# Differential attention in a two-layer kernel: two heads' value products interleaved in the two column halves, transposes and products in two parts, one order per engine

## The reference, cut to what matters

```python
def _L1_attn_ref(x, Wq, Wkv, Wout, lambda_q1, ..., gamma):      # H = 8, D = 32, B = 4, T = 1024
    q = (x @ Wq).reshape(B, T, 2 * H, D).transpose(0, 2, 1, 3) * scaling
    k, v = jnp.split(x @ Wkv, 2, axis=-1)                        # k: 2H heads of 32, v: H heads of 64
    dots = jnp.einsum('bhqd,bhkd->bhqk', q, k)
    attn_w = jax.nn.softmax(dots, axis=-1).reshape(B, H, 2, T, T)
    attn_w = attn_w[:, :, 0] - lam * attn_w[:, :, 1]
    attn = jnp.einsum('bhqk,bhkd->bhqd', attn_w, v)
    rms = jnp.sqrt(jnp.mean(attn * attn, axis=-1, keepdims=True))
    attn = gamma * (attn / (rms + EPS)) * (1.0 - LAMBDA_INIT)
    return attn.transpose(0, 2, 1, 3).reshape(B, T, 2 * H * D) @ Wout
```

## Time and profile before

| | us |
|---|---|
| median of 3 runs | 2968.69 (2963.91 to 2975.45) |
| the profiled execution | 2971.7, of which 2969.5 are the span of the trace |
| mean granted clock of TensorE | 0.886 of 2.4 GHz |
| PE busy | 2382.1 (80% of the span) |
| DVE busy | 2111.1 (71%) |
| ACT busy | 1700.0 (57%) |
| POOL busy | 1430.3 (48%) |

### The profile page before, as it was taken

The page is one execution under the profiler, slowest core; times in us unless marked ns, Lnnn a source line. Parts: engine busy times, 40 slices in busy tenths (PEclk is TensorE's granted clock), DMA queues, the critical chain, the costliest instruction groups (busy, mean ns, idle before and its releaser), DMA issues.

```text
span 2969.5 us, 42353 instructions
## 1 busy us (share of the span) xinstructions
PE 2382.1 (80%) x15570; PEld 1714.4 (58%) x15570; DVE 2111.1 (71%) x3677; ACT 1700.0 (57%) x2627; POOL 1430.3 (48%) x1343
## 2 busy tenths in 40 slices
PE   2433887788596989999999999999998299758877
PEld 1101454455365656777777777777776267645675
DVE  4999879969788128888788888888886622463334
ACT  5443765666474438787778777877785124212432
POOL 0435234323434006558656766676568432464056
PEclk7555988789598999999999999999999699878988
DMA  3000000000000000110001100100000100000000
GB/s 102 0 0 0 1 1 1 1 1 18 0 1 1 22 1 23 25 29 22 18 16 29 25 18 17 28 23 18 19 23 1 43 1 1 1 15 1 1 1 15
DMA packets 32030, 42.03 MB, mean 14 GB/s; under 512 B 8897, under 2 KB 18130, under 8 KB 31442
## 3 DMA queue, kind: packets, MB, share of 16 engines
q1 hardware_dynamic: 31826, 39.34, 4.9%
HBM read 12.05 MB, written 2.10 MB: 5 GB/s over the span
## 4 chain that ended last, share of the span: by engine, by line
PE 54%; DVE 20%; ACT 10%; POOL 8%; issue 7%; SPq 0%; POOLq 0%; DMA 0%; DVEq 0%; ACTq 0%
PE ps L1137 11%; PE ps L863 6%; PE ps L1113 6%; PE ps L1124 6%; DVE MA L1279 3%; PE ps L792 3%; ACT HR L764 2%; PE ps L794 2%; PE ps L793 2%; PE ps L1934 2%; PE ps L1092 2%; DVE BIG L337 2%; ACT BIG L449 2%; DVE lnb L318 2%; DVE BIG L343 2%
## 5 line engine op out<-in xcount | busy, mean ns | idle before, releaser
L1279 DVE TENSOR_REDUCE MA<-ps 128x1 f32<-128x1024 f32 x512 | 623.3, 1221 | 180.3 <-PE ps L1113 167.5
L421 POOL TENSOR_TENSOR MA<-MA,BIG 128x1024 f32<-128x1024 f32 x128 | 299.2, 2359 | 544.3 <-DVE BIG L343 544.3
L1206 ACT ACTIVATE WB<-ps,MA 128x1024 f32<-128x1024 f32 x359 | 400.6, 1116 | 197.3 <-DVE MA L1279 197.3
L1137 PE MATMUL ps<-WB,MA 128*64 128x128 f32 x4096 | 505.7, 277 | 0.0
L1137 PEld LDWEIGHTS ps<-WB,MA 128*64 128x64 f32 x4096 | 443.5, 137 | 88.9 <-issue 87.8
L1113 PE MATMUL ps<-BIG 96*128 96x512 f16 x1024 | 312.7, 387 | 16.6 <-ACT WB L1206 13.7
L863 PEld LDWEIGHTS ps<-WB,HR 128*128 128x128 f32 x2304 | 291.8, 202 | 33.5 <-issue 16.4
L863 PE MATMUL ps<-WB,HR 128*128 128x128 f32 x2304 | 300.8, 288 | 8.7 <-DVE acc L708 8.5
L764 ACT ACTIVATE HR<-ps,b 128x512 f32<-128x512 f32 x288 | 190.4, 687 | 147.0 <-PE ps L794 146.1
L1213 ACT ACTIVATE WB<-ps 128x1024 f32<-128x1024 f32 x256 | 260.0, 1016 | 4.4 <-PE ps L1124 4.4
L1697 POOL TENSOR_TENSOR BIG<-MA,BIG 128x512 f32<-128x512 f32 x128 | 132.2, 1049 | 236.8 <-PE ps L1920 77.5
(11 more groups left out here) (297 smaller groups left out, 4858.4 us busy)
## 6 DMA issues: line engine op xcount, KB each, us to landing
BIG<-BIG SPq DMA_DIRECT2D x192, 64.0 KB, 2.0
BIG<-MA SPq DMA_DIRECT2D x192, 64.0 KB, 2.0
WB<-w_dram SPq DMA_DIRECT2D x1, 2304.0 KB, 14.9
X<-x_dram SPq DMA_DIRECT2D x4, 512.0 KB, 12.5
HR<-w_dram SPq DMA_DIRECT2D x1, 2048.0 KB, 9.5
out_dram<-X SPq DMA_DIRECT2D x4, 512.0 KB, 3.2
WB<-wqkv_dram SPq DMA_DIRECT2D x1, 1536.0 KB, 6.5
WB<-w_dram SPq DMA_DIRECT2D x2, 512.0 KB, 8.5
```

What stands on the lines that cost most here:

```text
L421: e.tensor_tensor(yy[:, c, :], yy[:, c, :], db[n % 2][c], ALU.add).then_inc(*p_my.up(b, n, c))
L1137: x = e.matmul(bank[6][64 * pp:64 * pp + 64, 0:128], V[(4 * b + g) % 2][:, k, 64 * pp:64 * pp + 64], DT[n % 2][:, 128 * k:128 * k + 128], ...
L1206: e.activation(P_of(n, s), ps[s][:, :], ACT.Exp, bias=L[:, 2 * s + pp:2 * s + pp + 1], scale=1.0, accum_out=L[:, 4 + 2 * s + pp:5 + 2 * s ...
L1279: e.tensor_reduce(L_of(n)[:, c:c + 1], ps[s][:, :], AX, ALU.max, negate=True).then_inc(*v_amx.up(n, s))
```

## The change

It has four parts. First, `weigh` now belongs to a pair: its 16 products are issued in two parts of four key tiles each, and within a part the product of head 0 (array columns 0 to 63) and that of head 1 (columns 64 to 127) alternate. The pieces `weigh0` and `weigh1` wait for the transposed maps of both units, the output of the pair before must have been copied ahead of `weigh0`, and the ring `DT` has four tiles. Second, `flip` is split into transposes 0 to 4, which wait for DVE's part of the difference, and 5 to 7, which wait for POOL's. Third, the ring of ten tiles becomes five for s = 0 and three for s = 1 (the other two tiles went to `DT`), and the exponential of (n, 1) now waits for both parts of the difference of n - 3. Fourth, the list is made from a table of times in units (`UNIT_AT`, `PREP_AT`), and each engine sorts it anew with offsets of its own (`LATE`). The number, shapes and types of all operations stay as they were.

```diff
-        N_UNITS, TL, W = 256, 4, 640
+        UNIT_AT = {"scores0": -0.16, "sums": 1.3, "scores1": 0.58, "gather": 6.98, "settle": 9.01, "flip0": 4.39,
+                   "flip1": 4.79, "weigh0": 5.63, "weigh1": 6.96, "difference": 3.04}
+        PREP_AT = 0.92
+        LATE = {"pe": {"scores1": -0.12, "flip0": -0.01, "flip1": -0.37, "weigh0": 0.71, "weigh1": 0.06,
+                       "settle": 0.03, "between": -0.22},
+                "act": {"scores0": 0.04, "scores1": 0.28, "flip1": -0.85, "gather": -0.04, "between": -0.28},
+                "dve": {"scores0": 0.09, "scores1": -0.1, "sums": -0.27, "settle": -0.04, "difference": 0.16,
+                        "between": -0.65},
+                "pool": {"sums": -0.48, "difference": -0.26, "between": -0.95}}
+        N_UNITS, W = 256, 640
...
-            for n in range(N_UNITS + 8):
-                if 0 <= n - 6 < N_UNITS and n % 2:
-                    order.append(("gather", n - 6))
-                if n < N_UNITS:
-                    b, g, i, pp = unit(n)
-                    if i == pp == 0:
-                        while ("v", b, g, 1) in [p for _, p in prep]:
-                            advance(n)
-                    order.append(("scores", n, 0))
-                if 0 <= n - 1 < N_UNITS and n % 2 == 0:
-                    order.append(("sums", n - 1))
-                if 0 <= n - TL < N_UNITS:
-                    order.append(("flip", n - TL))
-                if n < N_UNITS:
-                    order.append(("scores", n, 1))
-                if 0 <= n - 7 < N_UNITS and n % 2 == 0:
-                    order.append(("settle", n - 7))
-                    b, g, i, pp = unit(n - 7)
-                    if g == 3:
-                        settled[b] = i + 1
-                        if i == 0:
-                            t = tail(b)
-                            tails.append([b, t, next(t)])
-                if 0 <= n - TL - 1 < N_UNITS:
-                    order.append(("weigh", n - TL - 1))
-                if 0 <= n - 2 < N_UNITS:
-                    order.append(("difference", n - 2))
-                advance(n)
-                for _ in range(2 if n % 64 < 8 or n % 64 > 52 else 1):
-                    tail_piece(n % 2 == 1)
+            events = []
+            for n in range(N_UNITS):
+                events += [(n + UNIT_AT[what], x, (what[:-1], n, int(what[-1])) if what[-1] in "01" else (what, n))
+                           for x, what in enumerate(UNIT_AT) if n % 2 or what not in ("sums", "weigh0", "weigh1", "gather", "settle")]
+            for t, x, p in sorted(events + [(n + PREP_AT, 99, None) for n in range(N_UNITS + 9)]):
+                if p is None:
+                    n = int(t)
+                    advance(t, n)
+                    for _ in range(2 if n % 64 < 8 or n % 64 > 52 else 1):
+                        tail_piece(t, n % 2 == 1)
+                    continue
+                n = p[1]
+                b, g, i, pp = unit(n)
+                if p[0] == "scores" and i == pp == p[2] == 0:
+                    while ("v", b, g, 1) in [q for _, q in prep]:
+                        advance(t, n)
+                order.append((t, p))
+                if p[0] == "settle" and g == 3:
+                    settled[b] = i + 1
+                    if i == 0:
+                        g = tail(b)
+                        tails.append([b, g, next(g)])
             assert not prep
-            order.append(("end",))
+            order.append((t + 1, ("end",)))
             while tails:
-                tail_piece(True)
+                tail_piece(t + 2, True)
             return order
 
         ORDER = attention_order()
-        OPENING = ORDER[:ORDER.index(("scores", 0, 0))]
-        ORDER = ORDER[len(OPENING):]
+        first = [p for _, p in ORDER].index(("scores", 0, 0))
+        OPENING, ORDER = [p for _, p in ORDER[:first]], ORDER[first:]
+
+        def order_of(engine):
+
+            def at(x):
+                t, p = ORDER[x]
+                what = p[0] + str(p[2]) if p[0] in ("scores", "flip", "weigh") else p[0] if p[0] in UNIT_AT else "between"
+                return round(t + LATE[engine].get(what, 0), 3) if p[0] != "end" else t
+
+            return [ORDER[x][1] for x in sorted(range(len(ORDER)), key=lambda x: (at(x), x))]
...
-        t_as, t_at, t_aw, t_az = tick("t_as", N_UNITS, 2), tick("t_at", N_UNITS), tick("t_aw", N_UNITS), tick("t_az", PAIRS)
+        t_as, t_at, t_aw, t_az = tick("t_as", N_UNITS, 2), tick("t_at", N_UNITS), tick("t_aw", PAIRS, 2), tick("t_az", PAIRS)
...
-        P_ = ([WB[:, 6144 + 1024 * i:7168 + 1024 * i] for i in range(3)] + [WB[:, 1024 * i:1024 * i + 1024] for i in range(3)]
-              + [SEL[:, 2048 * i:2048 * i + 2048].bitcast(F32) for i in range(2)] + [WB[:, 5120:6144], BC[:, 0:2048].bitcast(F32)])
-        osl = [OS[:, 128 * i:128 * i + 128] for i in range(2)]
-        DT = [WB[:, 3072 + 1024 * i:4096 + 1024 * i] for i in range(2)]
+        P_ = [[WB[:, 6144 + 1024 * i:7168 + 1024 * i] for i in range(3)] + [WB[:, 5120:6144], BC[:, 0:2048].bitcast(F32)],
+              [WB[:, 1024 * i:1024 * i + 1024] for i in range(3)]]
+        weighed_ = [OS[:, 128 * i:128 * i + 128] for i in range(2)]
+        DT = ([WB[:, 3072 + 1024 * i:4096 + 1024 * i] for i in range(2)]
+              + [SEL[:, 2048 * i:2048 * i + 2048].bitcast(F32) for i in range(2)])
...
-            return P_[(2 * n + s) % 10]
+            return P_[s][n % len(P_[s])]
...
                 elif kind == "flip":
-                    n = p[1]
-                    e.wait_ge(*v_ad.at(n))
-                    if n:
-                        e.wait_ge(*a_at.at(n - 1))
-                    for k in range(8):
-                        if 128 * k == W:
-                            e.wait_ge(*p_ad.at(n))
+                    _, n, part = p
+                    if part == 0:
+                        e.wait_ge(*v_ad.at(n))
+                        if n:
+                            e.wait_ge(*a_at.at(n - 1))
+                    else:
+                        e.wait_ge(*p_ad.at(n))
+                    for k in range(W // 128) if part == 0 else range(W // 128, 8):
                         x = e.transpose(ps[2][:, 128 * k:128 * k + 128], P_of(n, 0)[:, 128 * k:128 * k + 128], ident[:, :])
-                    x.then_inc(*t_at.up(n))
+                    if part:
+                        x.then_inc(*t_at.up(n))
                 elif kind == "weigh":
-                    n = p[1]
-                    b, g, i, pp = unit(n)
-                    e.wait_ge(*a_at.at(n))
-                    if i == pp == 0:
-                        e.wait_ge(*a_av.at(b, g, 1))
-                    if pp == 0 and n:
-                        e.wait_ge(*a_ag.at(n // 2 - 1))
-                    elif n == 0:
-                        e.wait_ge(*v_fcb.at(NB - 1, 16))
-                    for k in range(8):
-                        x = e.matmul(bank[6][64 * pp:64 * pp + 64, 0:128], V[(4 * b + g) % 2][:, k, 64 * pp:64 * pp + 64],
-                                     DT[n % 2][:, 128 * k:128 * k + 128], start=k == 0, stop=k == 7)
-                    x.then_inc(*t_aw.up(n))
+                    _, n, part = p
+                    b, g, i, _ = unit(n)
+                    m = n // 2
+                    if part == 0:
+                        e.wait_ge(*a_at.at(n))
+                        if i == 0:
+                            e.wait_ge(*a_av.at(b, g, 1))
+                        if m:
+                            e.wait_ge(*a_ag.at(m - 1))
+                        else:
+                            e.wait_ge(*v_fcb.at(NB - 1, 16))
+                    for k in range(4 * part, 4 * part + 4):
+                        for pp in range(2):
+                            x = e.matmul(bank[6][64 * pp:64 * pp + 64, 0:128], V[(4 * b + g) % 2][:, k, 64 * pp:64 * pp + 64],
+                                         DT[(2 * m + pp) % 4][:, 128 * k:128 * k + 128], start=k == 0, stop=k == 7)
+                    x.then_inc(*t_aw.up(m, part))
                 elif kind == "settle":
                     m = p[1] // 2
                     e.wait_ge(*a_ag.at(m))
-                    e.transpose(bk[:, 0:128], osl[m % 2], ident[:, :]).then_inc(*t_az.up(m))
+                    e.transpose(bk[:, 0:128], weighed_[m % 2], ident[:, :]).then_inc(*t_az.up(m))
...
-                        e.wait_ge(*t_aw.at(16 * q - 17))
+                        e.wait_ge(*t_aw.at(8 * q - 9, 1))
...
-                    if n >= 5:
-                        if s == 0:
-                            e.wait_ge(*t_at.at(n - 5))
-                        else:
-                            e.wait_ge(*v_ad.at(n - 5))
-                            e.wait_ge(*p_ad.at(n - 5))
+                    if s == 0 and n >= 5:
+                        e.wait_ge(*t_at.at(n - 5))
+                    if s == 1 and n >= 3:
+                        e.wait_ge(*v_ad.at(n - 3))
+                        e.wait_ge(*p_ad.at(n - 3))
...
```

(34 more changed lines are left out.)

## The result

The changed kernel takes 2838.5 us (median of 4 runs, 2825.4 to 2841.2), beside 2966.3 us for the kernel before; the ratio is 0.956, with a 95% interval of 0.952 to 0.960. The forecast was 2837 us. The profiled execution has a span of 2834.0 us, 135.5 less than before, and the rows of the kernel after show where they went.

A forecast was written before the change was run, and what follows sets the result against it. The prediction took PE to bound the attention's body, with DVE next at 93% busy. From the profiled 2971.7 us, minus 136 for the body, plus 4 for the drain, gave 2839.7; the median lies 3.0 lower, so 2837 us, range 2780 to 2985.

The forecast's parts named there:

- PE as the bound before: Attention's body before the change: PE, busy 1119 of 1166 us (96%), is the slowest member of the ring.
- Part 1, the overlap: Products alternating in the column halves run in parallel: bursts of 1.05 us instead of 1.89, saving 215 us of PE time.
- What is next: Attention's body after the change: DVE becomes the bound at 93% busy, body 1030 us, saving 136 us.
- the clock: PE's granted clock in the attention's body: about 0.94 at 88% busy, given as the reason for staying below 96%.
- Part 2, the split transposes: Transposes on PE split by DVE's and POOL's parts of the difference: cost and gain nothing, still 0.88 us.
- Part 3, the rings: Exponential (n, 1) waits for the difference of n - 3: hidden, with half a unit (2 us) in time.
- wrong in the rings: Sign of failure: ACT line 1206 waits for POOL or DVE 1288, or PE waits for ACT over 50 us in total.
- Part 4, the orders: New order of PE's pieces in a pair: serves the ring and makes 93% thinkable, nothing extra counted.
- One longer drain, + 4 us: The last settle comes two units later (9 instead of 7), adding 4 us.
- B: Rival, chance 0.11: the column halves don't overlap, PE keeps 1119 us and its 96%, some 2972 us.
- C: Rival, chance 0.09: the array settles at each change of half, 0.09 us each, 161 us in all, 3133 us.
- A: Rival, chance 0.14: halves overlap, but the s = 1 wait or a slower clock eats part of the gain, 2905 us.

The follow-up runs named there:

- same_half: The changed kernel with both heads' alternating products sent to the same 64 array columns and PSUM partitions: 2934.8 us, ratio 0.989 to the kernel before.
- flip_whole: The changed kernel with the transposes in one part, all eight waiting for DVE's and POOL's parts of the difference: 2830.8 us, ratio 0.956 to the kernel before.
- before_rings: The kernel before with only the changed kernel's rings and their waits, products by unit, one order: 2960.1 us, ratio 0.999 to the kernel before.
- old_order: The changed kernel's alternating products, rings and split transposes in the previous kernel's order, one list, 32 products in one piece: 3012.4 us, ratio 1.016.
- pe_list: The changed kernel with all four engines walking PE's own list: 2923.0 us, ratio 0.986 to the kernel before.
- diff_later: The changed kernel with DVE's difference moved behind the maximum of s = 1 by one offset: 2898.8 us, ratio 0.979 to the kernel before.

## Why the prediction was right, step by step

**PE as the bound before:** right. Without the overlap PE is at 97% again (same_half), under new orders too.

**Part 1, the overlap:** right in kind and size. Predicted 215 us less of PE time, bursts of 1.05 us and a busy time near 290 us; measured 220, 1.09 (up to the last end) and 285.5. The page "TensorEngine Tiling (Array Packing)" of the Trainium skill, section Key Properties, says that different tiles load and multiply in parallel; the trace agrees, with two records in 0.33 us. The rule of the Trainium skill that loads pass matmuls only in another row group ("TensorE: Matmul & The Clock Gate", Part 3) would have given 2972 us. Here every load uses all 128 rows, and 16 loads took 0.85 us under the 1.09 us of their burst, so the measurement decides against the rule for column halves. One term was wrong though it did no harm: I had the weight loads one after the other, 0.05 us apart and "just enough". Only the first two of a burst lie 0.05 us apart; after them the step is 0.11, and 16 in a row take 1.72 us. They keep up because they too run in pairs.

**What is next:** right. DVE at 93% and a body of 1030 us were the forecast; it is 94% (970.7 / 1036), and from the first product to the last 1030.6 us. Two sizes inside this were off. DVE's own work grew by 13 us (957.5 to 970.7) and POOL's by 94 (767.7 to 861.9), which I had as constant; the last section shows why. And the clock, which I let fall to 0.94, stayed at 0.98 with PE 89% busy, so the reason that I gave for staying under 96% wasn't the real one; what DVE did wait for were PE's scores (34 us) and ACT's row sums (11 us). The 93% itself was a choice between 88% and 98% that came out well, not the result of a sum.

**Part 2, the split transposes:** right, nothing (flip_whole).

**Part 3, the rings:** right in the old order (before_rings). In the new one ACT's exponentials waited for POOL's part of the difference 11 times, 10.5 us in all, up to 1.8 us, so the margin that I gave as 2 us is used up now and then; on PE's list for all it was 35 times and 57.7 us. One of the signs that I gave for "wrong in the rings" did appear, PE waiting for ACT over 50 us: its matmuls of line 1125 waited 81 us for the exponentials. It was a poor sign. PE has slack now and must wait for somebody, and the sum came out all the same.

**Part 4, the orders:** this step failed. "I count nothing extra" took it that the gain would come with PE's time and the order merely serve it. The runs show: overlap in the old order 1.6% slower in one piece and 0.8% faster in two; orders without overlap 1.1% faster; both together 4.4%. The sum of the parts is 1.9%, so more than half of the gain exists only when both are there. (Part of this has a plain reason: with PE at 97% no order can bring much.) My number came out because I took DVE's utilisation, 93%, straight as the end state and so priced the orders into it without saying so. That the number is right is luck as far as this step goes. With PE's list for all engines the right number would have been 2923 us, and the text had no step from which to see that. "One longer drain, + 4 us" isn't visible at the end: what follows the last product took 677.8 us for 679.6 before. The cost is at the front, where the time from the first scores to the first product grew from 28.1 to 34.9 us. It was hidden by first scores that came 5.8 us earlier, at 1090.7 us; the variants of the changed kernel have them anywhere between 1081 and 1096 us, so I take this for chance.

**The rivals:** B and C are ruled out, since the mean step is 0.055 us and not 0.112 or more. C's price was not well founded: a fourth pair of scores in the earlier trace rows, with no burst before or behind it, took 0.55 us, so 0.54 against 0.45 doesn't show the price of a change of width. A named a gain that is eaten in the ring; in the changed kernel it isn't, but in old_order, pe_list and diff_later it is, in whole or in part.

## What to carry to other kernels

Products that fill half of TensorE's columns should be issued so that neighbours use different halves: here that doubled their pace, and merely standing near each other gave under half of it (95 of 220 us). But in a ring of engines that are all near 90% busy, as here, time freed on the bound is worth what the order lets through; price the order as a step of its own, by asking of each engine what it is doing at the moment when the bank comes free, and keep single pieces short against one turn of the ring. An operation moved to a less busy engine can cost more than it frees: here it took twice as long there and held a bank that a third engine needed.

## What the runs showed of the hardware that was not expected

DVE's difference and some of POOL's operations on SBUF don't run side by side; the one that starts second waits. The two-element product on POOL (line 1351 before, 1367 after) had a median of 197 ns before, 744 in the changed kernel, where DVE's difference starts directly behind the reciprocal that releases it, and 197 again in diff_later. The rows: engine, line, count: min/median/max ns, of the kernel after and of diff_later.

```profile
L1367 POOL TENSOR_TENSOR MA<-MA x128: 191/744/782, 1107.1 to 2139.1; 128x2 f32<-128x2 f32 x128
```

```profile
L1367 POOL TENSOR_TENSOR MA<-MA x128: 187/197/782, 1098.0 to 2192.0; 128x2 f32<-128x2 f32 x128
```

The product doesn't merely slow down. In the kernel after, 118 of the 128 products start while a difference runs, and every one of them ends 0.05 to 0.06 us after that difference. The difference gets no longer by it: with the product alone beside it, it takes 0.85 us. It is long where it starts itself in the first 0.8 us of POOL's sum of line 1379: all 104 such differences end 0.68 us behind that sum, whatever their start. In this timeline the sum runs from 1603.43 to 1604.43 us, the difference (alone 0.88 us) ends at 1605.11, and the product, which starts in between, ends at 1605.16:

```profile
1604.38 0.78 POOL L1367 TENSOR_TENSOR MA<-MA 128x2 f32<-128x2 f32 x1
...
1603.57 1.54 DVE L1304 SCALAR_TENSOR_TENSOR WB<-WB,MA 128x640 f32<-128x640 f32 x1
```

It isn't every pair of operations: in the kernel before, the difference took its 0.87 to 0.88 us in all 114 cases where it started 0.45 us or more after POOL's scaling of line 1360 and under it. Nor is it the order of POOL's queue, since the same product in the same queue takes 0.20 us in diff_later, where the difference starts later. These waits make up the growth of POOL's work: over all units the product took 91 us instead of 25 and the scaling (line 1376 after) 371 instead of 333. The differences took 267 us instead of 236, and DVE's maxima 18 us less in the body, which leaves DVE's 13.

The chosen order pays this price (about 0.12 us per difference on the mean, and half a us per pair on the product) and is faster than the one that avoids it.
